# Loading a mixture-of-experts tile as four strips, turned by VectorE instead of TensorE

## The reference, cut to what matters

```python
flat = x.reshape(T, D)                       # T = 4096, D = 128
probs = softmax(flat @ router_w.T)           # 8 experts
topk_p, topk_i = top_k(probs, 2)
topk_w = topk_p / topk_p.sum(-1)
for e in range(8):
    out += square(relu(flat @ w_fc[e].T)) @ w_proj[e].T * combine[:, e]   # 512 hidden
out += square(relu(flat @ shared_fc.T)) @ shared_proj.T
x = layernorm(x + out)
```

## Time and profile before

| what | us |
|---|---|
| median of 3 runs | 490.98 |
| lowest and highest of them | 490.75, 491.0 |
| span of the profiled execution | 498.7 |
| TensorE busy in that span (matmuls) | 453.9 |
| VectorE busy | 356.7 |
| ScalarE busy | 354.5 |
| GpSimd busy | 315.1 |

### The profile page before, as it was taken

How to read it: one execution, slowest core, us unless ns; L and a number is a source line. 1 busy time by engine, 2 the same in 40 slices (tenths; PEclk the granted TensorE clock), 3 DMA queues, 4 the chain that set the end, 5 groups by cost and what they waited for, 6 DMA issues and landing times.

```text
span 498.7 us, 7644 instructions
## 1 busy us (share of the span) xinstructions
PE 453.9 (91%) x2184; PEld 293.6 (59%) x2184; DVE 356.7 (72%) x873; ACT 354.5 (71%) x557; POOL 315.1 (63%) x285
## 2 busy tenths in 40 slices
PE   8997999999999988798898898489999999999983
PEld 5332444444344333455576675389999999899721
DVE  5898999999999999998688964353333333455246
ACT  3989999999999999815455555327667667566537
POOL 4754789999999999845566666604555455555421
PEclk9998999999999999989799999979999999999997
DMA  8031246654343434001111111131222222222095
GB/s 274 8 122 43 86 146 213 216 196 151 130 153 131 151 133 148 3 1 33 39 45 43 45 43 47 46 94 51 72 65 81 71 60 58 60 57 67 11 324 182
DMA packets 41193, 48.56 MB, mean 97 GB/s; under 512 B 5616, under 2 KB 25266, under 8 KB 41152
## 3 DMA queue, kind: packets, MB, share of 16 engines
q1 hardware_dynamic: 35792, 39.07, 23.8%
q0 software_dynamic: 5216, 8.70, 5.6%
q10 hardware_dynamic: 144, 0.31, 0.2%
HBM read 19.17 MB, written 29.11 MB: 97 GB/s over the span
## 4 chain that ended last, share of the span: by engine, by line
PE 40%; POOL 22%; DVE 16%; issue 8%; ACT 7%; DMA 2%; another core or an unknown queue 2%; DVEq 0%; POOLq 0%; SPq 0%; ACTq 0%
POOL memory_feat L495 17%; PE routed_ph L1500 13%; PE routed_po L1513 12%; PE dispatch_sph L998 4%; PE dispatch_spo L1008 3%; POOL memory_feat L503 2%; DVE memory_prod L769 2%; DVE memory_y_raw L778 2%; POOL memory_prod L518 2%; PE memory_nsum L620 1%; ACT finish_xo L1714 1%; PE routed_px L1488 1%; PE dispatch_plr L969 1%; DVE memory_feat L769 1%
## 5 line engine op out<-in xcount | busy, mean ns | idle before, releaser
L495 POOL TENSOR_TENSOR memory_feat<-memory_feat,memory_p_tok 128x1024 f32<-128x1024 f32 x64 | 125.9, 2063 | 17.1 <-ACT memory_feat L390 14.2
L620 PE MATMUL memory_nsum<-memory_feat,tri 128*128 128x512 f32 x256 | 118.1, 604 | 6.3 <-ACT memory_last_rows L403 2.4
L1476 POOL DMA_INDIRECT pick_scratch<-routed_ob,routed_xg x71 | 71.6, 1008 | 75.1 <-DVE routed_ob L1597 56.7
L1192 POOL DMA_INDIRECT table_scratch<-dispatch_xrow,dispatch_slot x64 | 61.9, 967 | 40.9 <-PE dispatch_sph L998 18.9
L620 PEld LDWEIGHTS memory_nsum<-memory_feat,tri 128*128 128x128 f32 x256 | 47.8, 192 | 65.1 <-issue 56.2
L1546 ACT ACTIVATE routed_rel<-routed_ph 128x512 f32<-128x512 f32 x71 | 42.3, 597 | 47.7 <-PE routed_ph L1500 46.7
L1513 PE MATMUL routed_po<-routed_w2c,routed_hid 128*128 128x128 f32 x568 | 71.3, 276 | 1.2 <-DVE routed_ob L1597 0.7
L1500 PE MATMUL routed_ph<-routed_xs,routed_w1c 128*128 128x256 f32 (+1 forms) x368 | 71.1, 337 | 1.2 <-DVE routed_w2c L1583 0.9
L1597 DVE TENSOR_SCALAR routed_ob<-routed_po,routed_xg 128x128 f32<-128x128 f32 x71 | 22.6, 347 | 69.2 <-issue 49.6
L769 DVE TENSOR_TENSOR memory_prod<-memory_nsum,memory_query 128x1024 f32<-128x1024 f32 x58 | 68.8, 1216 | 1.9 <-PE memory_nsum L620 1.8
L1513 PEld LDWEIGHTS routed_po<-routed_w2c,routed_hid 128*128 128x128 f32 x568 | 67.0, 192 | 1.9 <-issue 1.1
(11 more groups left out here) (192 smaller groups left out, 694.6 us busy)
## 6 DMA issues: line engine op xcount, KB each, us to landing
table_scratch<-memory_blank SPq DMA_DIRECT2D x68, 260.0 KB, 2.6
finish_pick<-pick_scratch SPq DMA_DIRECT2D x16, 256.0 KB, 6.0
routed_xg<-table_scratch SPq DMA_DIRECT2D x25, 130.0 KB
w<-w_up SPq DMA_DIRECT2D x9, 256.0 KB, 2.7
w<-w_down SPq DMA_DIRECT2D x9, 256.0 KB, 3.1
x_tok<-x SPq DMA_DIRECT2D x4, 512.0 KB, 3.7
out<-finish_xo SPq DMA_DIRECT2D x7, 256.0 KB, 2.3
routed_xg<-table_scratch SPq DMA_DIRECT2D x21, 65.0 KB
```

Source lines behind the costliest of these rows:

```text
L495: nc.gpsimd.tensor_tensor(v, v, pv, ALU.mult).then_inc(wfeat_done, 1)
L620: last = nc.tensor.matmul(nsum[:, o:o + 512], tri[:], feat[:, i % U, h, q * 512:(q + 1) * 512], start=True, stop=True)
L1192: nc.gpsimd.indirect_dma_start(out=table, in_=xrow[:, r, n, :], in_offset=None, out_offset=bass.IndirectOffsetOnAxis(ap=slot[:, r, n:n + 1 ...
L1476: nc.gpsimd.indirect_dma_start(out=pick_dram, in_=ob[:, u, h, :], in_offset=None, out_offset=bass.IndirectOffsetOnAxis(ap=xg[:, t % XU, h, ...
```

## The change

A tile is no longer loaded as rows. Four DMAs each take a strip of 32 features of all its rows and lay it on 32 partitions, so that the 32 x 32 blocks of the tile stand where VectorE's block transpose, one instruction for the tile, makes of them the tile with features on partitions. VectorE writes `xs` directly. TensorE's transposes, the PSUM tile `px` and ScalarE's copies are gone. The row number and the weight of each row come in a fifth DMA (`mark`, 8 bytes a row).

SyncE issues two strips, two tiles ahead of the marks in its program, and the marks. ScalarE issues the other two: those of tiles 0 to 2 at the start, then those of tile t+3 at the end of round t, behind the Squares of tile t+1. Each of the two engines reads the tile's first row into a register of its own. VectorE turns tile t+2 in round t, between the weights of t+3 and the scaling of t; at the start it copies the weights of three tiles and then turns two.

```diff
     XU = 8
+    SQ = 32
+    STRIPS = D // SQ
+    BY_ACT = 2
+    AHEAD = 3
     with ExitStack() as c:
...
         def sem(name):
...
-        xg = sb("xg", [P, XU, HALVES, RW])
+        xb = sb("xb", [P, XU, ROWS])
+        mark = sb("mark", [P, XU, HALVES, RW - D])
         xs = sb("xs", [P, 2, ROWS])
...
         po = ps("po", [P, FC * P])
-        px = ps("px", [P, FC * P])
         loaded = [sem(f"loaded{u}") for u in range(XU)]
+        marked = [sem(f"marked{u}") for u in range(XU)]
         scattered = [sem(f"scattered{u}") for u in range(U)]
         turned = sem("turned")
-        x_kept = sem("x_kept")
         w_ready = sem("w_ready")
...
         def sync(sp):
...
-            def load(t, u):
+            def strips(t):
                 if t == FULL:
...
                 if not early(t, XU):
+                    sp.wait_ge(turned, t - XU + 1)
+                n = height(t)
+                rows = table[bass.ds(first, n * P), :]
+                for j in range(BY_ACT):
+                    sp.dma_start(xb[j * SQ:(j + 1) * SQ, t % XU, 0:n * P].rearrange("a (i b) -> a i b", b=SQ),
+                                 rows[:, j * SQ:(j + 1) * SQ].rearrange("(i a) b -> a i b", a=SQ)).then_inc(loaded[t % XU], 16)
+
+            def marks(t, u):
+                first = sp.value_load(start[0:1, t:t + 1], min_val=0, max_val=TABLE - ROWS)
+                if not early(t, XU):
                     sp.wait_ge(scattered[u], passes(t - XU))
                 n = height(t)
-                sp.dma_start(xg[:, t % XU, 0:n], table[bass.ds(first, n * P), :].rearrange("(h p) c -> p h c", p=P)
-                             ).then_inc(loaded[t % XU], 16)
-            tiles(lambda: None, load)
+                rows = table[bass.ds(first, n * P), :]
+                sp.dma_start(mark[:, t % XU, 0:n], rows[:, D:].rearrange("(h p) c -> p h c", p=P)).then_inc(marked[t % XU], 16)
+
+            def front():
+                strips(0)
+                strips(1)
+
+            def body(t, u):
+                if not beyond(t, 2):
+                    strips(t + 2)
+                marks(t, u)
+            tiles(front, body)
...
             def body(t, u):
...
                         out=pick_dram, in_=ob[:, u, h, :], in_offset=None,
-                        out_offset=bass.IndirectOffsetOnAxis(ap=xg[:, t % XU, h, D:D + 1].bitcast(U32), axis=0),
+                        out_offset=bass.IndirectOffsetOnAxis(ap=mark[:, t % XU, h, 0:1].bitcast(U32), axis=0),
                         bounds_check=2 * NTOK - 1, oob_is_err=False).then_inc(scattered[u], 16)
...
         def tensor(pe):
-            def turn(t, u):
-                pe.wait_ge(loaded[t % XU], 16 * (t // XU) + 16)
-                if not early(t, 1):
-                    pe.wait_ge(x_kept, t)
-                for h in range(height(t)):
-                    last = nc.tensor.transpose(px[:, h * P:(h + 1) * P], xg[:, t % XU, h, 0:D], ident[:])
-                last.then_inc(turned, 1)
-
             def up(t, u):
                 s = u % 2
-                pe.wait_ge(x_kept, t + 1)
+                pe.wait_ge(turned, t + 1)
                 pe.wait_ge(w_ready, t + 1)
...
             def front():
-                turn(0, 0)
-                turn(1, 1)
                 up(0, 0)
...
             def body(t, u):
...
                     up(t + 1, (u + 1) % U)
-                if not beyond(t, 2):
-                    turn(t + 2, (u + 2) % U)
                 down(t, u)
...
         def scalar(act):
-            def keep_x(t, u):
-                act.wait_ge(turned, t + 1)
-                if not early(t, 2):
-                    act.wait_ge(up_done, parts(t - 1))
-                n = height(t) * P
-                nc.scalar.copy(xs[:, u % 2, 0:n], px[:, 0:n]).then_inc(x_kept, 1)
-
             def rectified(t, u):
...
+            def load(t):
+                if t == FULL:
+                    act.wait_ge(dis.tabled, 2)
+                first = act.value_load(start[0:1, t:t + 1], min_val=0, max_val=TABLE - ROWS)
+                if not early(t, XU):
+                    act.wait_ge(turned, t - XU + 1)
+                n = height(t)
+                rows = table[bass.ds(first, n * P), :]
+                for j in range(BY_ACT, STRIPS):
+                    act.dma_start(xb[j * SQ:(j + 1) * SQ, t % XU, 0:n * P].rearrange("a (i b) -> a i b", b=SQ),
+                                  rows[:, j * SQ:(j + 1) * SQ].rearrange("(i a) b -> a i b", a=SQ)).then_inc(loaded[t % XU], 16)
+
             def front():
-                keep_x(0, 0)
-                keep_x(1, 1)
+                act.wait_ge(dis.tabled, 1)
+                for r in range(2):
+                    act.wait_ge(dis.sent[r], 16 * NT)
+                for t in range(AHEAD):
+                    load(t)
                 rectified(0, 0)
...
             def body(t, u):
...
                     rectified(t + 1, (u + 1) % U)
-                if not beyond(t, 2):
-                    keep_x(t + 2, (u + 2) % U)
                 if not beyond(t, 1):
                     squared(t + 1, (u + 1) % U)
+                if not beyond(t, AHEAD):
+                    load(t + AHEAD)
             tiles(front, body)
...
         def vector(dve):
...
+            def turn(t):
+                dve.wait_ge(loaded[t % XU], 16 * STRIPS * (t // XU + 1))
+                if not early(t, 2):
+                    dve.wait_ge(up_done, parts(t - 1))
+                n = height(t) * P
+                nc.vector.transpose(xs[:, t % 2, 0:n], xb[:, t % XU, 0:n]).then_inc(turned, 1)
+
             def front():
...
                     weights(t, t)
+                for t in range(2):
+                    turn(t)
...
             def body(t, u):
...
                     weights(t + 3, (u + 3) % U)
+                if not beyond(t, 2):
+                    turn(t + 2)
                 dve.wait_ge(down_done, t + 1)
+                dve.wait_ge(marked[t % XU], 16 * (t // XU + 1))
                 if not early(t, U):
...
                 for h in range(height(t)):
-                    last = nc.vector.tensor_scalar(ob[:, u, h, :], po[:, h * D:(h + 1) * D], xg[:, t % XU, h, D + 1:D + 2],
+                    last = nc.vector.tensor_scalar(ob[:, u, h, :], po[:, h * D:(h + 1) * D], mark[:, t % XU, h, 1:2],
                                                    None, ALU.mult)
...
                            scattered=[(scattered[t % U], passes(t)) for t in range(TILES - U, TILES)],
-                           x_kept=x_kept, rel_done=rel_done, banks=parts(TILES), kept=kept)
+                           rel_done=rel_done, banks=parts(TILES), kept=kept)
...
 def finish(nc, outer, rou, ident, y_all, eps, warm, pick_dram, out):
...
             shared(7)
-            pe.wait_ge(rou.x_kept, TILES)
             shared(6)
```

More of the change, by code:

```diff
@@ L60 @@
 DispatchStage = namedtuple("DispatchStage", "sync scalar gpsimd tensor vector sent tabled experts_in")
-RoutedStage = namedtuple("RoutedStage", "sync scalar gpsimd tensor vector scattered x_kept rel_done banks kept")
+RoutedStage = namedtuple("RoutedStage", "sync scalar gpsimd tensor vector scattered rel_done banks kept")
 FinishStage = namedtuple("FinishStage", "sync scalar gpsimd tensor vector")
```

## The result

The changed kernel takes 501.94 us (median of 4 runs, 501.43 to 503.18) against 490.99 (490.75 to 491.26): ratio 1.023, 95% interval 1.021 to 1.025. It is 11 us slower; the forecast was 498.6. The profiled execution took 503.18 us, with a span of 501.3.

What follows compares the result with a forecast made beforehand. Full rounds were taken as TensorE-bound, half rounds as ScalarE's and TensorE's together. Front +2.4, clock +1.7, full -5.2, half +8.7 sum to +7.6: 506.3 on the profiled span, 498.6 us carried to the median; range 489 to 512.

Steps and rivals of the forecast that it cites:

- The full rounds, -5.2: Routed stage, full tiles: removing TensorE's turnings saves 5.2 us, a round falling from 3.74 to 3.52.
- slack that it put at 0.30 a pair: Full tiles: ScalarE's load loop takes 6.74 us against two TensorE rounds of 7.04, so it just fits.
- The half rounds, +8.7: Half tiles: ScalarE's load loop takes 5.11 us for two rounds, 2.55 a round instead of 2.00; +8.7 over twenty.
- I take 1.6: Half tiles: a strip lands 1.6 us after ScalarE's second issue, from today's half load of 1.53.
- does not wait: Half tiles: the next tile's Relu, behind the load on ScalarE's queue, is due later than ScalarE's 2.20 occupancy.
- The front, +2.4: Start of routed stage: VectorE copies three tiles' weights before turning tile 0, moving first up from 332.55 to 334.94.
- the clock, +1.7: First two ups: TensorE's clock falls in the new idle gap, and half of their 3.69 us takes as long again.
- The strips are there by then: Front: tile 0's strips have landed before VectorE's first turn, with SyncE's first issue at 327.14.
- ScalarE's load is cheap: Faster rival: ScalarE's load is cheap or lands early, half-tile pair below 4.35 us; 486.6 us, chance 0.15.
- Full rounds wait too: Rival: second strips land 0.75 later, full rounds 3.75 lose the 5.2, half tiles +16.2; 511.5 us, chance 0.13.
- The pieces are dear: Rival: each of 1,280 pieces costs 60 ns, DMA bounds full tiles at 4.8 us; 529 us, chance 0.07.
- VectorE's floor of 2.04: Half tiles: VectorE's chain of scaling, weight copies and turn keeps a round from falling under 2.04 us.

Runs made afterwards that it cites:

- The doubled read: Changed kernel with the register read ahead of the Square, edited so ScalarE reads the tile's start twice from tile 3 on: 514.15 us, 1.0475.
- before: The kernel without the change: 490.99 us, median.
- the profile shown: First profile of the unchanged kernel, read by the prediction: span 498.7 us.
- the second profile: The unchanged kernel profiled again, no edit: ratio 0.9987, profiled span 491.7.
- after: The changed kernel: 501.94 us against 490.99, ratio 1.023; profiled span 501.3.
- the long pieces: Changed kernel with the same bytes and four DMAs a tile, but whole rows in pieces of 512 bytes instead of 128, tiles not turned: 500.71 us, 1.0187.
- twelve buffers: Changed kernel with five tiles ahead, early register read and SyncE reading once, plus 12 strip and mark buffers instead of 8: 487.08 us, 0.990.
- two traces: Traces of the changed kernel (501.94 us) and of its variant where ScalarE reads each tile's start early and twice (514.15 us).

## Why the prediction came out as it did

**The full rounds, -5.2: right.** 3.74 fell to 3.51 (forecast 3.52), -4.97 over the stretch; the prediction's own product, 23 x 0.22 + 2 x 0.11, is 5.28. The slack that it put at 0.30 a pair was there and somewhat larger, 0.58 less the 0.06 that is left at least, from two errors that partly cancel: the first issue comes 0.31 behind the start of the second Square and not 0.77, because the read runs beside it, and the landing took 2.25 on the mean and not 2.04. The doubled read used the slack up.

**The half rounds, +8.7: right mechanism, wrong size, +14.5.** The loop over two rounds is what set them: one tile of lead more undid it, a shorter read shortened it, a longer one lengthened it. Mean steps of the 18 loops from tile 26 on, from start to start, against the prediction's:

| step | forecast | measured |
|---|---|---|
| up to Relu | 1.20 | 1.27 |
| Relu to Square | 0.64 | 0.63 |
| Square to first issue | 0.77 | 0.70 |
| first to second issue | 0.45 | 0.53 |
| second issue to turn | 1.60 | 2.00 |
| turn to up | 0.45 | 0.42 |
| two rounds | 5.11 | 5.54 |

The step that failed is "I take 1.6" for the landing. I had read it from the windows in which a load's bytes move; what counts is the time until the waiting engine starts, 1.82 in the median, and the mean, 2.00, is raised most by the two strips that meet an instruction load (1.85 without them). Up to Relu is longer because, against the prediction's "does not wait", some Relus wait for ScalarE's issues. Ten pairs at 0.43 are 4.3 of the missing 5.8. The rest is the base: before's half tiles took 42.4 in the profile shown and 40.7 in the second. That TensorE's clock would not fall here was right: from 414 to 468 the granted clock was 1.00.

**The front, +2.4, and the clock, +1.7: wrong, 0.04 together.** "The strips are there by then" was read from an execution with an idle stretch of 6 us; in the second profile and in after the loads are the last to arrive. The clock did fall, as forecast, but it falls in before too, so nothing was added. That 498.6 came within 3.3 of 501.94 is in part luck: these 4.1 us too many hid most of the 5.8 too few.

**The other costs.** SyncE was said to take 2.75 a tile (2.77) and to hide it: true here, and wrong as soon as the rounds shorten. *ScalarE's load is cheap* falls: in half tiles the read and the issues cost what was forecast. *Full rounds wait too* falls for this kernel, but was near: an issue 0.6 later was enough. *The pieces are dear* falls by the long pieces. Of the rule in "DMA: Bandwidth & Descriptors", Specifications, of the Trainium skill, this case shows at most the 0.37 in a full tile's landing. VectorE's floor of 2.04 a half round was too high: with twelve buffers it was 1.98 behind the first round.

## What to carry to other kernels

When an engine that computes also issues loads, write the loop down: compute of tile s, issue, landing, consumer, compute of tile s + n; divide by n. If that exceeds the round, raise n before anything else. Price a landing from issue to the start of the waiting instruction, and leave room for one that is 1.5 us late. A profile's front with all engines idle for microseconds should be taken again before costs are read from it.

## What the runs showed of the hardware

An instruction load (queue q8, one packet of 16 KB, 1.0 to 1.4 us) held up one engine of a strip in flight, and the strip came 1.0 to 1.6 us later than the median, in six of six late landings of two traces. In after's routed stage there are eight such packets. Two begin 1.8 and 1.3 us behind ScalarE's first issue of a tile and go with a late strip; the others begin 2.2 us or more behind it or outside a load, and the landings there are 2.0 to 2.6. Pieces of 128 bytes against 512 cost a half tile's landing nothing that shows (2.00 and 1.98) and a full tile's 0.37 (2.27 and 1.90). VectorE's block transpose took 0.31 us for 128 columns and 0.45 for 256.
